# Fusing four transformer layers on one core: the second full attention's keys computed ahead of their stage and kept in DRAM

## The chip, the cores and the metric

The kernel runs on one core of a Trainium2 chip. The metric is device time in microseconds (us) of that core; the median of three runs stands below. The engines are TensorE (PE in the rows, its weight loads PEld), VectorE (DVE), ScalarE (ACT), GpSimd (POOL) and SyncE (SP), which only issues DMAs. ACTq and SPq are the DMA queues that ACT and SP issue to.

## The reference

Four layers follow each other over `x` of 8 rows (batch) x 128 tokens x 256 features, each an attention to a fixed context and a feed-forward block, with a residual sum and a layer norm ahead of both:

```python
x = x + _L0_xattn_ref(_layernorm(x), ctx_2048, ...)   # first cross attention, over 256 feature positions, 16 heads
x = x + _L0_ffn_ref(_layernorm(x), ...)               # first mixture of 8 experts, 2 chosen
x = x + _L1_xattn_ref(_layernorm(x), ctx_2048, ...)   # second cross attention
x = x + _L1_ffn_ref(_layernorm(x), ...)               # quantised feed-forward
x = x + _L2_xattn_ref(_layernorm(x), ctx_2048, ...)   # full attention, 16 heads of 128
x = x + _L2_ffn_ref(_layernorm(x), ...)               # low-rank mixture
x = x + _L3_xattn_ref(_layernorm(x), ctx_2048, ...)   # attention to memory
x = x + _L3_ffn_ref(_layernorm(x), ...)               # grouped attention, then the second mixture of experts

def _L2_xattn_ref(inputs_q, inputs_kv, Wq, Wk, Wv, Wo):
    q = (inputs_q @ Wq).reshape(b, sq, H, HD) * (1.0 / np.sqrt(HD))
    k = (inputs_kv @ Wk).reshape(b, skv, H, HD)
    v = (inputs_kv @ Wv).reshape(b, skv, H, HD)
    attn = jax.nn.softmax(jnp.einsum('bqhd,bkhd->bhqk', q, k), axis=-1)
    return jnp.einsum('bhqk,bkhd->bqhd', attn, v).reshape(b, sq, H * HD) @ Wo
```

The line that the change is about is `k = inputs_kv @ Wk`. Its `inputs_kv` is the context, an input of the whole program: these keys depend on nothing that is computed before them. They are 1024 tokens x 2048 columns in float32, 8.4 MB.

## The kernel before

Every engine has one program, written out by hand, that runs in order; engines meet at semaphores (`wait_ge`). PSUM is the tile `P` with eight banks of 512 words a lane. `big1`, `big2`, `big3` and `small` are areas of SBUF that each stage lays out anew; `X` holds the residual rows, `XN` the normalised ones, `XNT` and `CT` the transposed rows and the transposed context. The stages, in order of time:

- **First cross attention** (0 to 195 us). `s0_sp` loads and stacks, `s0_pe`, `s0_act`, `s0_dve` and `s0_pool` walk over `STEPS`. A step is one head `h` of 16 of one row `n` of 8. In each step PE writes `scores(n, h)` into bank 0 or 1 (L305), DVE takes their maximum (L480), and 24 steps later (`LEAD = H + 8`) PE computes the same product the other way round, `turned(m, g)` (L323), ACT takes its exponential (L556), and every fourth step PE weighs the values with it, `weigh` (L341), and once a row places the sums, `place` (L353). In the first 24 steps there are thus only `scores`, besides `project` (L286, L287) at h = 2 and `values` (L295) at h = 6. The queries and keys of a row go out to DRAM split in three bf16 parts (`split_out`, L256) and come back as stacks of lanes (`s0_stack`, L247 and L249, twelve DMAs a row); mask lanes follow (`s0_extra`, L234), and one row of ones goes through `SCR1` (L531, L534). The maxima go back to the stacks in `max_rows` (L516, DMAs that ACT issues).
- **Routing of the first mixture** (195 to 226 us). `s1_pe` turns the normalised rows and forms the gate logits (L148, L157), DVE chooses experts (L714 to L967), PE counts ranks (`ranks_pe`, L804 to L809), turns the shares (L827), forms the bias rows (L831) and the slots (`slots_pe`, L814). Then the gathers, `turn` (L848), and the experts' loop, `up` (L858) and `down` (L868), 23 blocks with 2 MB of weights each, to about 430 us.
- **Second cross attention and its feed-forward** (to about 541 us).
- **Full attention with the low-rank mixture and the attention to memory** (`s47_pe`, 541 to about 860 us). One step `m` of 32 is one group of four heads (`b, g = divmod(m, 4)`). In step m PE runs, in this order: `scores4(m + 1)` (L1807), `queries4(m + 2)` (L1782), `turn_probs4(m)` (L1815), `keys4(m + 2)` (L1789), a piece for a later layer's row (`second`, L1841 and L1865), `output4(m - 1)` (L1834), `values4(m + 1)` (L1798), another piece (`third`, L1884 and others), `weigh4(m)` (L1822). ACT copies queries and keys out of PSUM (`copy_qk4`, L2116 and L2117), takes exponentials (L2124) and copies the turned probabilities (L2132); DVE finds maxima, scales (L2310) and copies the values (L2295) and the weighed sums (L2315), and keeps the residual rows and layer norms (L126 to L134).
- **Grouped attention** (the same function's second loop, to about 1150 us), of the same shape with other pieces, and then the second mixture.

A float32 matrix product of the source shows as two MATMUL records. A **pair**, below, is the keys of one head (128 columns) for 512 tokens (four of the eight rows): two products, one for each half of the 256 features, into one bank. 16 heads and two groups of rows make 32 pairs.

## Time and profile before

| | us |
|---|---|
| median of 3 runs | 1279.91 (1278.62 to 1280.27) |
| span of the profiled execution | 1275.9 |
| PE busy | 1085.1 (85% of the span) |
| DVE busy | 704.5 (55%) |
| ACT busy | 503.4 (39%) |
| POOL busy | 319.7 (25%) |

The span is that of the one execution that was profiled, from its first to its last instruction. It is 4.0 us under the median, which is what lies around the span; differences worked out in the span are carried over to the median as they are. PE's busy time is a union of overlapping records, so a stretch in which PE is busy all the time may be read as one in which it is the bound. The granted TensorE clock is given as a share of full speed (1.0 is 2.4 GHz, 0.5 is 1.2 GHz).

### The profile page before, as it was taken

The page shows a single profiled execution, that of the slowest core. Times are in us where ns is not written, and L with a number is a line of the kernel's source. Part 1 is how long each engine was busy: PE and PEld are TensorE (multiplying, and loading weights), DVE is VectorE, ACT ScalarE, POOL GpSimd, SP SyncE. Part 2 cuts the span into 40 slices and gives each one's busy share as a digit, 9 for nine tenths or more (in the row PEclk, how much of TensorE's full clock was granted, in tenths as well). Part 3 has the DMA queues.
Part 4 walks back from the last instruction along what each step waited for, and adds up shares of the span by engine and source line. Part 5 has one row for each costly group of instructions (what it writes and reads, how often), then busy time and mean ns, then how long its engine had stood idle before and what let it go on. Part 6 is the DMA issues. An engine that isn't in the chain of part 4 may idle for free.

```text
span 1275.9 us, 20612 instructions
## 1 busy us (share of the span) xinstructions
PE 1085.1 (85%) x7154; PEld 830.8 (65%) x7170; DVE 704.5 (55%) x1700; ACT 503.4 (39%) x1785; POOL 319.7 (25%) x440
## 2 busy tenths in 40 slices
PE   1788886999996788799999999996788999984784
PEld 0355444899995566588888888884555666653463
DVE  5777756212223788854554455555656666665334
ACT  0165561233231466644333333342445555542121
POOL 5544211122322355510000000002222222210562
PEclk9699996899997799999999999998989999997797
DMA  6443207899882070000000000040000000000785
GB/s 185 133 129 110 84 32 237 301 327 334 315 322 79 10 256 1 2 28 20 1 1 1 1 1 1 34 133 1 1 1 9 5 6 5 5 4 24 238 250 177
DMA packets 59731, 121.31 MB, mean 95 GB/s; under 512 B 9049, under 2 KB 37481, under 8 KB 53713
## 3 DMA queue, kind: packets, MB, share of 16 engines
q1 hardware_dynamic: 52217, 106.62, 25.0%
q0 software_dynamic: 4416, 12.06, 2.8%
q10 hardware_dynamic: 2996, 1.32, 0.4%
q8 instruction: 58, 0.95, 0.3%
q14 instruction: 44, 0.36, 0.1%
HBM read 107.29 MB, written 12.49 MB: 94 GB/s over the span
## 4 chain that ended last, share of the span: by engine, by line
PE 60%; DVE 17%; issue 8%; ACT 7%; DMA 4%; POOL 2%; SPq 1%; another core or an unknown queue 1%; ACTq 0%; DVEq 0%; POOLq 0%
PE P L858 6%; PE P L868 6%; PE P L1789 4%; PE P L1782 4%; PE P L1834 4%; PE P L1798 4%; ACT big L2213 3%; DVE small L480 2%; PE P L1927 2%; PE P L1807 2%; PE P L1822 2%; PE P L1933 2%; PE P L1978 2%; ACT big L2181 2%; PE P L341 1%
## 5 line engine op out<-in xcount | busy, mean ns | idle before, releaser
L139 POOL TENSOR_TENSOR lrs<-lve,mhalf 128x1 f32<-128x1 f32 x64 | 36.6, 572 | 364.5 <-DVE lve L130 332.4
L480 DVE TENSOR_REDUCE small<-P 128x2 f32<-128x512 f32 x128 | 83.3, 681 | 38.9 <-PE P L305 38.2
L2124 ACT ACTIVATE big<-P,small 128x128 f32<-128x128 f32 x128 | 45.2, 366 | 145.0 <-DVE small L2304 145.0
L897 ACT ACTIVATE big<-P,big 128x128 f32<-128x128 f32 x184 | 52.5, 368 | 125.3 <-PE P L858 112.4
L556 ACT ACTIVATE big<-P 128x512 f32<-128x512 f32 x128 | 72.0, 598 | 58.6 <-PE P L323 53.6
L858 PE MATMUL P<-big 128*128 128x128 f32 x736 | 88.2, 279 | 0.1
L858 PEld LDWEIGHTS P<-big 128*128 128x128 f32 x736 | 86.1, 196 | 1.0 <-DMA big<-b_w 0.5
L868 PE MATMUL P<-big 128*128 128x256 f32 x368 | 83.1, 379 | 0.0
L305 PE MATMUL P<-big 90*128 90x256 bf16 x256 | 54.9, 303 | 32.9 <-DMA big<-scr_qk 17.5
L2295 DVE COPY big<-P 128x512 f32<-128x512 f32 x32 | 22.1, 692 | 107.2 <-PE P L1798 107.2
L999 DVE COPY big<-P 128x256 f32<-128x256 f32 x23 | 9.8, 425 | 125.3 <-PE P L868 125.3
L2443 DVE TENSOR_TENSOR big<-P,big 128x512 f32<-128x512 f32 x40 | 27.6, 690 | 87.3 <-ACT big L2181 87.2
L868 PEld LDWEIGHTS P<-big 128*128 128x128 f32 x368 | 68.2, 190 | 8.4
L1978 PE MATMUL P<-big 128*128 128x256 f32 x256 | 64.1, 396 | 0.4 <-DVE big L2498 0.4
L1782 PE MATMUL P<-XNT,big 128*128 128x128 f32 x512 | 62.6, 275 | 0.0
L1789 PE MATMUL P<-CT,big 128*128 128x128 f32 x512 | 62.4, 275 | 0.0
L1927 PE MATMUL P<-big,XNT 128*128 128x512 f32 x128 | 61.4, 603 | 1.2 <-DVE big L2445 1.2
L305 PEld LDWEIGHTS P<-big 90*128 90x128 bf16 x256 | 20.3, 103 | 62.7 <-DVE small L480 29.1
L1933 PEld LDWEIGHTS P<-idf,big 128*128 128x128 f32 x288 | 35.7, 147 | 39.0 <-issue 22.7
L1834 PE MATMUL P<-big 128*128 128x256 f32 x256 | 60.6, 380 | 0.0
L1798 PE MATMUL P<-big,CT 128*128 128x512 f32 x128 | 60.2, 592 | 0.0
L1782 PEld LDWEIGHTS P<-XNT,big 128*128 128x128 f32 x512 | 59.7, 192 | 0.2 <-issue 0.2
(388 smaller groups left out, 2584.2 us busy)
## 6 DMA issues: line engine op xcount, KB each, us to landing
big<-b_w SPq DMA_DIRECT2D x23, 1028.0 KB
big<-b_w SPq DMA_DIRECT2D x23, 1024.0 KB
big<-scr_qk SPq DMA_DIRECT2D x96, 96.0 KB
big<-i_wgu SPq DMA_DIRECT2D x23, 352.0 KB
big<-moe_y SPq DMA_DIRECT2D x16, 256.0 KB, 4.2
big<-i_wd SPq DMA_DIRECT2D x23, 176.0 KB
scr_qk<-big SPq DMA_DIRECT2D x8, 384.0 KB
moe_x<-XN SPq DMA_DIRECT2D x16, 128.0 KB
```

Source lines behind the costliest of these rows:

```text
L305: t = pe.matmul(P[:, h % 2, c * D:c * D + D], QS[n % 3][0:90, h, c * 128:c * 128 + 128], KS[n % 3][0:90, h, :], start=True, stop=True)
L480: dve.tensor_reduce(negM[:, h, :], P[:, h % 2, :].rearrange("p (c s) -> p c s", c=2), AX.X, ALU.max, negate=True).then_inc(a_max, 1)
L556: act.activation(ER[:, g % 8], P[:, second_bank(i), :].rearrange("p (c t) -> p c t", c=2), ACT.Exp).then_inc(a_e, 1)
L858: m = pe.matmul(P[:, 2 * (j % 2) + f // 4, f % 4 * 128:f % 4 * 128 + 128], w1x[j % 3][:, k * F0 + f * 128:k * F0 + f * 128 + 128], xgT[j % ...
L868: m = pe.matmul(P[:, 6 + j % 2, 0:D], hT[j % 2][:, f, :], w2x[j % 3][:, f, :], start=(f == 0), stop=(f == FC - 1))
L1782: pe.matmul(P[:, 0, j * T:j * T + T], e_wqk[:, g, 0, k, j * 128:j * 128 + 128], XNT[:, k, b * T:b * T + T], start=(k == 0), stop=(k == KD ...
L1789: t = pe.matmul(P[:, 1, j * T:j * T + T], e_wqk[:, g, 1, k, j * 128:j * 128 + 128], CT[:, k, b * T:b * T + T], start=(k == 0), stop=(k == ...
L1798: t = pe.matmul(P[:, 2, :], CT[:, k, b * T:b * T + T], e_wvs[:, g, k, :], start=(k == 0), stop=(k == KD - 1))
L1834: t = pe.matmul(P[:, 7, 0:D], e_o[:, j, :], e_wos[:, 4 * g + j, :], start=(g == 0 and j == 0), stop=(g == 3 and j == 3))
L1927: t = pe.matmul(P[:, 0, :], XNT[:, k, b * T:b * T + T], h_wqs[:, g, k, :], start=(k == 0), stop=(k == KD - 1))
L1933: t = pe.transpose(P[:, bank, j * T:j * T + T], src[:, j, :], idf[:, :])
L1978: t = pe.matmul(P[:, 7, 0:D], h_o[:, j, :], h_wos[:, 4 * g + j, :], start=(g == 0 and j == 0), stop=(g == 3 and j == 3))
```

## The change

The keys of the full attention are no longer computed in their stage (`keys4` and the second copy of `copy_qk4` are gone). They are computed in 32 pairs at the start of the program, copied from PSUM to one of four slots in `XNT` (`k_out`) by ACT (`key_take`), stored from there to a DRAM tensor `KEYS` by a DMA that ACT issues (`key_store`, 256 KB in pieces of 512 bytes), and read back by SP as one 1 MB tile a row (`key_row`) into two buffers. The pairs stand at four places of PE's program: 8 ahead of the first `scores`, 12 as halves in the first 24 steps, 6 as halves at h = 5 and h = 10 of the rows 2 to 7, 3 behind the gate logits and 3 ahead of the first `turn`. A pair waits for the copy of an earlier one out of its bank (`k_ev`), a copy for the store of four pairs before it (`k_st`). Some semaphores are used twice, under new names with an offset (`k_pe` is `e_y`, `k_ev` is `f_ex`), which is why the rows below show these names.

To make room, other work is moved. The transposed context is loaded at the start and not with the first mixture's constants. The loads of the later rows of `x`, of the context, of the mask and of `selm` move behind: half of `x` to ACT's queue, behind the first key store, and the rest to SP's, between the store of a row's parts and the wait for it (`s0_behind`), together with the mask lanes of rows 1 and 2, which ACT issued before. In the full attention the queries have two SBUF buffers in place of one for queries and one for keys; the output weights of the grouped attention are loaded last.

```diff
+        k_wts = big1[:, 12288:16384].rearrange("p (g k n) -> p g k n", g=4, k=KD)
+        k_out = [XNT[:, s // 2, 512 * (s % 2):512 * (s % 2) + 512] for s in range(4)]
+        KEYS = nc.dram_tensor("keys_t", (B, 128, 4, 4, T), F32, kind="Internal").ap()
+        KP, K0, K1, K2 = 32, 8, 20, 26
+        def key_place(p):
+            g, rest = divmod(p, 8)
+            return g, rest // 4, rest % 4
+        def key_bank(p):
+            return 2 + p % 2 if p < K1 else 5 if p < K2 else (2, 3, 0, 0, 7, 6)[p - K2]
+        def key_weights(eng, g):
+            eng.dma_start(k_wts[:, g], e_wk.rearrange("(k p) n -> p k n", p=128)[:, :, 512 * g:512 * g + 512]
+                          ).then_inc(k_w[g], 16)
+        def key_take(act, p):
+            act.wait_ge(k_pe, p + 1)
+            if p >= 4:
+                act.wait_ge(k_st[p % 4], 16 * (p // 4))
+            act.activation(k_out[p % 4], P[:, key_bank(p), :], ACT.Copy).then_inc(k_ev, 1)
+        def key_store(act, p):
+            g, r, j = key_place(p)
+            act.wait_ge(k_ev, p + 1)
+            act.dma_start(KEYS[4 * r:4 * r + 4, :, g, j].rearrange("b p t -> p b t"),
+                          k_out[p % 4].rearrange("p (b t) -> p b t", b=4)).then_inc(k_st[p % 4], 16)
+        def key_part(pe, p, lo, hi):
+            g, r, j = key_place(p)
+            if lo == 0:
+                if p % 8 == 0:
+                    pe.wait_ge(k_w[g], 32 if g == 0 else 16)
+                if p == 4:
+                    pe.wait_ge(k_ct, 16)
+                if K1 <= p < K2:
+                    pe.wait_ge(k_ev, p)
+                elif 2 <= p < K1:
+                    pe.wait_ge(k_ev, p - 1)
+                elif p == K2 + 3:
+                    pe.wait_ge(k_ev, p)
+            for k in range(KD):
+                t = pe.matmul(P[:, key_bank(p), lo:hi], k_wts[:, g, k, 128 * j:128 * j + 128],
+                              CT[:, k, 512 * r + lo:512 * r + hi], start=(k == 0), stop=(k == KD - 1))
+            if hi == 512:
+                t.then_inc(k_pe, 1)
+        def late_pair(n, h):
+            if 2 <= n < B and h in (5, 10):
+                return K1 + n - 2, h // 10
+            return None
...
+            sp.dma_start(X[:, 2:4, :], x_cbt[:, 2:4, :]).then_inc(ld_x, 16)
+            ctx_t = ctxT.rearrange("(k p) n -> p k n", p=128)
+            sp.dma_start(CT[:, :, 0:512], ctx_t[:, :, 0:512]).then_inc(k_w[0], 16)
+            key_weights(sp, 0)
+            sp.dma_start(CT[:, :, 512:NT], ctx_t[:, :, 512:NT]).then_inc(k_ct, 16)
...
+            if n == 1:
+                sp.dma_start(TMf[:, 2 * D:], rows(mask.rearrange("b d -> (b d)").rearrange("(a n) -> a n", a=1)[:, 2 * D:])
+                             ).then_inc(a_ldm, 16)
+                sp.wait_ge(a_exd, 32)
+            if n in (1, 2):
+                for half in range(2):
+                    s0_extra(sp, n, half)
+            if n == 1:
+                key_weights(sp, 2)
+            if n == 2:
+                sp.dma_start(CX[:, 4:8, :], ctx.rearrange("b c t -> c b t")[:, 4:8, :]).then_inc(ld_c2, 16)
+                sp.dma_start(selm, a_sel).then_inc(a_ldm, 16)
+                key_weights(sp, 3)
...
+            for p in range(K0):
+                key_part(pe, p, 0, 512)
...
+                if step < LEAD:
+                    key_part(pe, K0 + step // 2, D * (step % 2), D * (step % 2) + D)
+                if late_pair(n, h) is not None:
+                    p, u = late_pair(n, h)
+                    if n + 2 < B and h == 5:
+                        pe.wait_ge(a_qb, n + 3)
+                    key_part(pe, p, D * u, D * u + D)
...
+            key_take(act, 0)
+            key_store(act, 0)
+            act.dma_start(X[:, 4:8, :], x.rearrange("b c t -> c b t")[:, 4:8, :]).then_inc(ld_x2, 16)
+            key_take(act, 1)
+            key_store(act, 1)
+            key_weights(act, 1)
             act.wait_ge(a_exd, 32)
-            for n in range(3):
-                for half in range(2):
-                    s0_extra(act, n, half)
+            for p in range(2, K0):
+                if p in (2, 4):
+                    s0_extra(act, 0, p // 2 - 1)
+                key_take(act, p)
+                key_store(act, p)
...
+                if step < LEAD and step % 2:
+                    key_take(act, K0 + step // 2)
+                    key_store(act, K0 + step // 2)
+                if 2 <= n < B and h == 11:
+                    key_take(act, late_pair(n, 10)[0])
+                if 2 <= n < B and h == 13:
+                    key_store(act, late_pair(n, 10)[0])
...
+            rows_logits_pe(pe, 1, gw, (b_ld, 80), b_lt)
+            for p in range(K2, K2 + 3):
+                key_part(pe, p, 0, 512)
...
+            for p in range(K2 + 3, KP):
+                key_part(pe, p, 0, 512)
             pe.wait_ge(b_acc, 4)
             turn(0)
             turn(1)
+            pe.wait_ge(k_ev, KP)
             up(0)
...
+        def key_row(sp, b):
+            if b >= 2:
+                sp.wait_ge(e_s, 4 * (b - 2) + 4)
+            sp.dma_start(e_kr[b % 2], KEYS[b]).then_inc(k_rd[b % 2], 16)
         def s4_sp(sp):
             sp.wait_ge(xn_ready, 3 * B)
-            for w, src in enumerate((e_wq, e_wk)):
-                for g in range(4):
-                    sp.dma_start(e_wqk[:, g, w], src.rearrange("(k p) n -> p k n", p=128)[:, :, 512 * g:512 * g + 512]
-                                 ).then_inc(e_ld, 16)
+            for signal in k_st:
+                sp.wait_ge(signal, 16 * KP // 4)
+            wq4 = e_wq.rearrange("(k p) n -> p k n", p=128)
+            sp.dma_start(e_wqs[:, 0], wq4[:, :, 0:512]).then_inc(e_ld, 16)
+            key_row(sp, 0)
+            for g in range(1, 4):
+                sp.dma_start(e_wqs[:, g], wq4[:, :, 512 * g:512 * g + 512]).then_inc(e_ld, 16)
             for g in range(4):
                 sp.dma_start(e_wvs[:, g], e_wv.rearrange("(k p) n -> p k n", p=128)[:, :, 512 * g:512 * g + 512]
                              ).then_inc(e_ld, 16)
             sp.dma_start(e_wos, e_wo.rearrange("(h p) d -> p h d", p=128)).then_inc(e_ld, 16)
+            key_row(sp, 1)
...
-            def keys4(m):
-                b, g = divmod(m, 4)
-                for j in range(4):
-                    for k in range(KD):
-                        t = pe.matmul(P[:, 1, j * T:j * T + T], e_wqk[:, g, 1, k, j * 128:j * 128 + 128],
-                                      CT[:, k, b * T:b * T + T], start=(k == 0), stop=(k == KD - 1))
...
+                if g == 0:
+                    pe.wait_ge(k_rd[b % 2], KRD0 + 16 * (b // 2) + 16)
...
-                if m + 2 < NM:
-                    keys4(m + 2)
...
-                act.activation(e_q.rearrange("p j t -> p (j t)"), P[:, 0, :], ACT.Copy)
-                act.activation(e_k.rearrange("p j t -> p (j t)"), P[:, 1, :], ACT.Copy).then_inc(e_qkT, 1)
+                if m >= 2:
+                    act.wait_ge(e_s, m - 1)
+                act.activation(e_q[m % 2].rearrange("p j t -> p (j t)"), P[:, 0, :], ACT.Copy).then_inc(e_qkT, 1)
```

The opening, PE, from its first product on, before. L286 and L287 are `project`, L305 is `scores`:

```order
L286 MATMUL P<-XN,small 128x256 [waits a_ld,xn_ready]
L287 MATMUL P<-CX,small 128x256
L286 MATMUL P<-XN,small 128x256 [waits a_qb,xn_ready]
L287 MATMUL P<-CX,small 128x256
L305 MATMUL P<-big 128x256 [waits a_stk00]
L305 MATMUL P<-big 128x256 x3
L305 MATMUL P<-big 128x256 [waits a_max]
```

and with the change, where L368 and L369 are `project`, L387 is `scores` and L259 a key product:

```order
L368 MATMUL P<-XN,small 128x256 [waits a_ld,xn_ready]
L369 MATMUL P<-CX,small 128x256
L368 MATMUL P<-XN,small 128x256 [waits a_qb,xn_ready]
L369 MATMUL P<-CX,small 128x256
L259 MATMUL P<-CT,big 128x512 [waits c_ld]
L259 MATMUL P<-CT,big 128x512 x3
L259 MATMUL P<-CT,big 128x512 [waits f_ex]
L259 MATMUL P<-CT,big 128x512
L259 MATMUL P<-CT,big 128x512 [waits f_ex]
L259 MATMUL P<-CT,big 128x512
L259 MATMUL P<-CT,big 128x512 [waits f_ex,i_ld]
L259 MATMUL P<-CT,big 128x512
```

Between the second `project` and the first `scores` there are now the 16 products of eight pairs (the rows shown are the first four of them), and each pair from the third on waits for `f_ex`, the count of copies.

The opening, ACT, before (L504 and L505 copy the projections, L524 and L525 store the mask parts, L234 is `s0_extra`):

```order
L504 ACTIVATE big<-P,small 128x256 [waits a_qkf,a_qk]
L505 ACTIVATE big<-P,small 128x256
L524 DMA scr_e<-big 8x4608 [waits a_exs]
L525 DMA scr_e<-big 8x4608
L234 DMA big<-scr_e 18x8x256 [waits a_exd]
L234 DMA big<-scr_e 18x8x256 x11
L531 DMA scr<-big 3x4096 [waits a_one]
L534 DMA big<-scr 3x4096 [waits a_exd]
```

and with the change (L235 is `key_take`, L241 `key_store`, L311 `s0_extra`):

```order
L623 DMA scr_e<-big 8x4608
L235 ACTIVATE XNT<-P 128x512 [waits e_y]
L241 DMA keys_t<-XNT 128x4x128 [waits f_ex]
L626 DMA X<-x 128x4x256
L235 ACTIVATE XNT<-P 128x512 [waits e_y]
L241 DMA keys_t<-XNT 128x4x128 [waits f_ex]
L227 DMA big<-e_wk 128x2x512
L311 DMA big<-scr_e 18x8x256 [waits a_exd]
L311 DMA big<-scr_e 18x8x256
L235 ACTIVATE XNT<-P 128x512 [waits e_y]
L241 DMA keys_t<-XNT 128x4x128 [waits f_ex]
L235 ACTIVATE XNT<-P 128x512 [waits e_y]
```

ACT's copies of the third pair and of all later ones stand behind its wait for `a_exd` and behind the mask lanes; the last of the eight stores is directly ahead of the store of ones and its wait.

One step of the full attention, PE, before, from `scores4` to `weigh4` (names in the section above):

```order
L1807 MATMUL P<-big 128x128 x4
L1782 MATMUL P<-XNT,big 128x128 x8
L1815 MATMUL P<-idf,big 128x128 x4
L1789 MATMUL P<-CT,big 128x128 x8
L1865 MATMUL P<-idf,big 128x128
L1834 MATMUL P<-big 128x256 x4
L1798 MATMUL P<-big,CT 128x512 x2
L1890 MATMUL P<-big 128x256
L1822 MATMUL P<-big 128x128 x4
```

and with the change, the same step:

```order
L1953 MATMUL P<-big 128x128 x4
L1932 MATMUL P<-XNT,big 128x128 x8
L1962 MATMUL P<-idf,big 128x128 x4
L2012 MATMUL P<-idf,big 128x128
L1981 MATMUL P<-big 128x256 x4
L1941 MATMUL P<-big,CT 128x512 x2
L2037 MATMUL P<-big 128x256
L1969 MATMUL P<-big 128x128 x4
```

The eight products of `keys4` are gone from between `turn_probs4` and the piece behind it; the other work of the step is in the same order.

## Rows read from the trace of the kernel before

**Rows 1.** The page's head.

```profile
span 1275.9 us, 20612 instructions
```

**Rows 2.** Windows: length; busy us (x instructions) of each engine; granted clock; DMA share; GB/s.

```profile
8.00:14.00 6.00, 4.09 (x8) 2.35 (x8) 5.86 (x10) 1.59 (x5) 2.55 (x3) 1.00 1.00 294
14.00:30.00 16.00, 0.00 (x0) 0.00 (x0) 7.57 (x21) 0.29 (x1) 11.65 (x11) 1.00 0.54 165
...
95.50:113.70 18.20, 15.72 (x145) 9.67 (x145) 13.88 (x28) 10.19 (x21) 8.96 (x14) 1.00 0.35 106
625.00:850.00 225.00, 225.00 (x1546) 196.07 (x1545) 116.59 (x345) 79.91 (x303) 13.00 (x27) 1.00 0.05 15
905.00:1145.00 240.00, 215.56 (x992) 143.91 (x1004) 156.05 (x355) 127.40 (x592) 51.78 (x87) 0.99 0.01 4
```

**Rows 3.** Groups by line: shape, count; busy us, mean ns; idle before.

```profile
L1789 PE MATMUL P<-CT,big 128*128 128x128 f32 x512 | 62.4, 275 | 0.0
...
L1798 PE MATMUL P<-big,CT 128*128 128x512 f32 x128 | 60.2, 592 | 0.0
```

**Rows 4.** Timeline, full attention: start, length, engine, line [idle before it].

```profile
707.61 1.95 PE L1789 MATMUL P<-CT,big 128*128 128x128 f32 x16
...
709.13 0.61 ACT L2132 ACTIVATE big<-P 128x512 f32<-128x512 f32 x1
...
709.39 0.27 PE L1865 MATMUL P<-idf,big 128*128 128x128 f32 x1
...
713.38 1.05 PE L1822 MATMUL P<-big 128*128 128x128 f32 x8
...
716.74 0.41 DVE L134 TENSOR_SCALAR XN<-X,lmv,lrs 128x256 f32<-128x256 f32 x1
...
719.39 0.38 PE L1841 MATMUL P<-idf,XN 128*128 128x128 f32 x2
```

**Rows 5.** Timeline, the opening.

```profile
12.35 1.06 PE L287 MATMUL P<-CX,small 128*128 128x256 f32 x2
...
16.41 0.39 SPq L256 DMA_DIRECT2D scr_qk<-big  x1
...
21.25 0.81 SPq L247 DMA_DIRECT2D big<-scr_qk  x1
...
21.68 8.18 ACTq L234 DMA_DIRECT2D big<-scr_e  x12
...
30.89 1.03 PE L305 MATMUL P<-big 90*128 90x256 bf16 x4 [17.47 <-DMA big<-scr_qk]
...
37.87 0.47 ACT L504 ACTIVATE big<-P,small 128x256 f32<-128x256 f32 x1 [23.58 <-DMA big<-scr]
```

**Rows 6.** Timeline, PE: the first `turned`, and `scores` at either clock.

```profile
56.34 0.61 PE L323 MATMUL P<-big 93*128 93x256 bf16 x2 [0.53 <-DMA big<-small]
...
63.61 0.38 PE L305 MATMUL P<-big 90*128 90x256 bf16 x2
63.83 0.38 PE L323 MATMUL P<-big 93*128 93x256 bf16 x2
```

**Rows 7.** Windows, the stretch around them.

```profile
55.00:60.00 5.00, 4.23 (x19) 2.43 (x20) 4.73 (x8) 2.05 (x4) 4.71 (x6) 0.50 0.45 132
```

**Rows 8.** Timeline, PE: `place` in a row of the steady part.

```profile
77.52 1.99 PE L353 MATMUL P<-big,small 128*128 128x256 f32 x8 [0.73 <-ACT big L540]
```

**Rows 9.** Timeline, PE: the routing of the first mixture.

```profile
199.10 1.66 PE L148 MATMUL P<-small,XNT 128*128 128x8 f32 x8
...
205.69 0.23 PE L804 MATMUL P<-big,small 128*128 128x64 bf16 x1 [4.93 <-DVE big L728]
...
224.78 1.23 PE L848 MATMUL P<-idf,big 128*128 128x128 f32 x4 [5.26 <-DMA big<-moe_x,big]
...
226.05 5.84 PE L858 MATMUL P<-big 128*128 128x128 f32 x32
...
231.94 3.74 PE L858 MATMUL P<-big 128*128 128x128 f32 x32
```

More of the change, by code:

```diff
@@ L884, in s1_act @@
         def s1_act(act):
+            for i in range(4):
+                act.wait_ge(k_st[i], 16 * len(range(i, K2, 4)))
             transposes_act(act, 1)
             gates_act(act, 0)
+            for p in range(K2, K2 + 3):
+                key_take(act, p)
+                key_store(act, p)
             act.wait_ge(b_cT, 1)
@@ L890, in s1_act @@
             t.then_inc(b_cTs, 1)
+            for p in range(K2 + 3, KP):
+                key_take(act, p)
+                key_store(act, p)
             for j in range(NB):
@@ L976, in s1_dve @@
             shares_of(dve, 0, 0.0)
-            step, weights_of = route_dve(dve, b_pos, POS0, b_rank, RANK0, b_ld, 128)
+            step, weights_of = route_dve(dve, b_pos, POS0, b_rank, RANK0, b_ld, 112)
             weights_of()
@@ L1712, in build @@
         CLEAR = 6
+        ld_x2, FLD0 = f_ld, 16
+        ld_c2, MLD0 = m_ld, 16
+        a_ldm, HLT0 = h_lt, 32
+        k_w, CLD0, ELD0, HLD0, HLD20 = [c_ld, e_ld, h_ld, h_ld2], 32, 16, 16, 16
+        k_ct, ILD0 = i_ld, 16
+        k_pe, EY0 = e_y, KP
+        k_ev, FEX0 = f_ex, KP
+        k_rd, KRD0 = [ld_c, ld_id], 16
+        h_ld3, HLD30 = a_ldv, 48
         def again(eng, sems):
@@ L1990, in turn_fed @@
                     t.then_inc(tb_pe, 1)
-            pe.wait_ge(e_ld, 208)
+            pe.wait_ge(e_ld, ELD0 + 144)
             pe.wait_ge(tb_ev, TURNED[B - 1])
             queries4(0)
-            keys4(0)
             output2(B - 1)
@@ L2001, in s47_pe @@
             queries4(1)
-            keys4(1)
             for m in range(NM):
@@ L2658, in build @@
         i_w = [sem("i_w0"), sem("i_w1"), i_z] + b_w
-        IW0 = [0] * 3 + [32 * len(range(u, NB, 3)) for u in range(3)]
+        IW0 = [16 * KP // 4] * 3 + [32 * len(range(u, NB, 3)) for u in range(3)]
         i_xs = b_xg + [a_stk[2][0], a_stk[2][1], e_max, e_bias, e_rz, e_pn]
         NG = len(i_xg)
+        k_st, MY0 = i_w[:3] + [m_y], 16 * KP // 4
         IXS0 = [16 * len(range(u, NB, 4)) for u in range(4)] + [0] * 6
```

108 lines of the change are left out of this document (63 added, 45 removed).

## The prediction, made before the changed kernel was run

> **What bounds the kernel now.** I read the windows first, stage by stage, and for each asked whether PE is ever idle. In the full attention it is not: of the 225 us from 625 to 850 PE is busy for 225.00, at the full clock, with DVE at 116.59 and ACT at 79.91 [rows 2]. Whatever is taken from PE there comes off the end, until another engine's chain is late. The grouped attention, of the same shape, is the warning: PE is busy for 215.56 of 240 us [rows 2], so there such chains do show. In the first cross attention PE is busy for 15.72 us of a row of 18.20, DVE for 13.88 [rows 2]; no engine is the bound alone, and they hand the path to each other. Ahead of it PE does nothing from 14 to 30 us [rows 2] and waits 17.47 us for the first stacks [rows 5], and in the routing it waits 4.93 us for DVE and 5.26 us for the first gather [rows 9]. The change moves PE work from the stage without holes to the places with holes. The sum is what it takes off less what does not fit in the holes.
>
> **The full attention: keys4 gone.** Its groups of records show 62.4 us for 512 [rows 3], 1.95 us a step, but the last record's tail overlaps what follows. From start to start the keys take 709.39 - 707.61 = 1.78 us [rows 4], and 32 steps give 57.0 us. What could be late when they no longer lie between `turn_probs4` and the rest? I moved the later rows of the step forward by 1.78 and looked at who feeds them. `weigh4`, at 713.38, would start at 711.60; it needs ACT's copy L2132, done at 709.13 + 0.61 = 709.74, 1.9 us to spare [rows 4]. The piece at 719.39 would start at 717.61; its input is the layer norm's L134, done at 717.15, 0.46 us to spare [rows 4]. What stands ahead of `turn_probs4` keeps its distance from it. ACT loses a copy a step. The read of a key row (1 MB, 8 KB pieces) is released five steps ahead of its use, some 40 us; at the 294 GB/s that the full share of 8 to 14 us moves it takes 3.6 us, and DMA is at a share of 0.05 in this stage [rows 2]: nothing. I allow 2.5 us for pieces that come late now and for the first two steps, where `scores4(1)` stands right behind the queries that it needs. **Term: -54.5** (bounds -57, and -29 as worked out in the first rival).
>
> **What a pair costs.** Products of 512 columns take 60.2 us for 64 [rows 3], less a tail of 0.16 a pair as above: 1.72 us a pair. A half of 256 columns I take at half of it. All this holds at full clock, and twice as much at half.
>
> **The opening: 20 pairs.** The second `project` ends at about 13.2 us [rows 5], and the weights and the first half of the context (1.3 MB behind 0.9 MB, at 294 GB/s) are there by 12 or 13. Eight pairs take 13.8 us at full clock, and the hole up to 30.89 [rows 5] is 17.7. But ACT gates them: its third copy stands behind the wait for the mask parts (21.68 before [rows 5]) and two mask-lane DMAs of 0.68 each (8.18 for 12 [rows 5]), so the fifth pair starts at about 24.5 and the eighth ends at about 32. First `scores`: 1.3 us later than before. Then 24 steps of 0.22 us for `scores` (63.61 to 63.83 [rows 6]), twelve pairs and 2.6 us of `project` and `values` (six 256-column products' worth at 0.43): 28.5 us of PE work, which DVE's reductions do not limit. Into this falls one wait: the copy of the ninth pair stands behind the store of ones and its return. Before, that took from the end of the mask lanes at 29.86 to 37.87 [rows 5], 8.0 us; now it begins at about 33, so PE, which wants that bank at about 38, waits until about 42. The 24 steps end at 65 in place of 56.34 [rows 6]: +8.7. Against this, the clock. Before, the first `turned` takes 0.61 us for what takes 0.38 later, and the window around it is at a granted 0.50 [rows 6, 7]; with PE at work without a hole from 13 us on I expect full clock there, which gives back 2 us. DMA: the mask, `x` and context loads move, but some 8.4 MB (5.2 of stores, 2 of weights, 1 of context) are new ahead of 65 us, 28 us of all 16 engines at 294 GB/s; the stretch to 65 goes from about half busy (0.54 in 14 to 30 [rows 2]) to 0.9. I take 2 us for it. **Term: +9** (bounds +3, all the stalls hidden, to +20).
>
> The Trainium skill, DMA: Bandwidth & Descriptors, section "Issuing engines are not separate DMA queues", says that DMAs of ACT and SP run on the same 16 engines and interleave, so a second issuing engine saves issue time only. No row here shows two queues at a full share together; by it the stores slow the stacks of SP's queue (the second rival), and were the queues apart, the term would be +7.
>
> **Six late pairs.** 10.3 us of PE work in six rows. The half at h = 10 stands where `place` waits 0.73 us for ACT [rows 8] and costs 0.1 to 0.2; the half at h = 5 waits for ACT's `queries_keys`, and behind that ACT issues the three DMAs of `max_rows`, which PE has to wait out anyway. PE has 18.20 - 15.72 = 2.5 us a row idle [rows 2] for 1.72. ACT's copy and store issue (1.1 us) fall where DVE is late. Between nothing and 10.3 I take **+4**, nearer to nothing because of the idle time.
>
> **The routing.** Three pairs (5.2 us) start when the logits end, at 199.10 + 1.66 = 200.8, and ranks start at 205.69 [rows 9]: +0.3 to +1. Three more stand ahead of the first `turn`, where PE waits 5.26 us for the gather [rows 9], a hole for 5.2 us at full clock, 10.3 at half. But `up` took 5.84 us there [rows 9], at half clock at first, against 3.74 for the 32 records of the next block [rows 9]; warmed, it gives 2 us back. **Term: +1** (bounds -1, +6). Six stores (1.6 MB) beside the experts' weights: **+0.5** (0 to 3). ACT's waits for `k_st` at stage borders find the stores landed.
>
> **Sum.** -54.5 + 9 + 4 + 1 + 0.5 = -40. On the span: 1275.9 [rows 1] to about 1236; on the median, 4.0 us above it: **1240**. The terms' likely errors together are some 10 us: 1228 to 1252.
>
> **Rivals.**
> 1. *The full attention finds a new bound.* If DVE's or ACT's chain limits it as in the grouped attention, PE is busy for 0.898 of the time (215.56 / 240 [rows 2]). Of the 309 us from 541 to 850, 252 of work remain; at 0.898 that is 281, so 28 of 57 come off: 1240 + 26 = 1266. For it: 0.46 us to spare above, and DVE's share rises to 116.59 / (225 - 41) = 0.63 [rows 2]. Against: the waits of the grouped attention are at rows that its other chain of queries brings. Chance 0.09.
> 2. *DMA bounds the opening.* If stores in 512-byte pieces move at half the 294 GB/s, 5.2 MB take 35 us in place of 18, and with about 30 of before and 10 of loads the 65 us become 76: +11, 1251, with late pairs at full price up to 1258. For it: the window at 8 to 14 us is already at share 1.00 [rows 2]. Chance 0.14.
> 3. *The clock stays at half in the first 24 steps* as in the window at 0.50, though PE was busy 4.23 of 5 us there [rows 7]: 28.5 us become 57, less 4 of stall: +25, 1265. Against: PE's stream is now denser than there, with products of 512 columns. The Trainium skill, TensorE: Matmul & The Clock Gate, Part 1, says that the throttled state is the default and activity releases it; by it this rival does not happen, and the trace agrees as far as the clock rises once `turned` joins `scores` [rows 6]. Chance 0.03.
> 4. *Slower than before: the four store slots.* The copy of pair p waits for the store of pair p - 4. A store of 384 KB landed in 21.25 - 16.41 = 4.8 us [rows 5]; four pairs take 6.9 us, so it is hidden. Were a store to take 25 us, sixteen pairs in four rounds would take 100, and the 24 steps end at 117: +58 for the opening, 1290. It decides from about 23 us on. Chance 0.04.
>
> **How the numbers follow.** Forecast 0.70 (1228 to 1252), rivals 0.09, 0.14, 0.03, 0.04. Range: 1226 to 1260, with the second rival in and the first, third and fourth (0.16) out, and a little below. A measurement tells 0.2% (2.6 us) from no change. Faster by more: all but the fourth and some mishap beyond the rows, 0.93; within 0.02; slower 0.05.
>
> **What would show it.** A step of the full attention 8.0 us long (9.7 before, 309 us for 32), PE without idle time; if it is idle before `turn_probs4` or the normalised rows, the first rival. The first `turned` near 65 us, at full clock, with waits of PE for ACT's copies near 24 and 40 us. A row of the steady part 0.7 us longer. Ranks within 1 us behind DVE's choice. A time over 1260 means a chain in the full attention that I did not see; one under 1226 that the opening's waits were no waits at all.

## The result and the profile after

| | before | with the change |
|---|---|---|
| median, us | 1280.25 (1278.62 to 1281.8) | 1271.65 (1268.04 to 1274.83), 5 runs |
| ratio | 1 | 0.9922 (0.9897 to 0.9946) |
| span of the profiled execution, us | 1275.9 | 1270.8 |

The change makes the kernel 0.8% faster: 8.6 us on the median, 5.1 us between the two profiled spans. Forecast was 40, and 1271.65 lies outside the range. The starts of a few first instructions in the two traces show where the difference arises. The shift is how much later an instruction comes than before, and its growth is what the stretch that ends there costs.

| first instruction of | before | after | shift | growth | forecast |
|---|---|---|---|---|---|
| `scores` | 30.9 | 40.1 | +9.2 | | +1.3 |
| `turned` | 56.3 | 90.1 | +33.8 | +33.8 | +9 |
| the gate logits | 194.9 | 233.2 | +38.3 | +4.5 | +4 |
| `up` | 226.1 | 268.6 | +42.5 | +4.2 | +1 |
| `queries4` | 540.0 | 583.0 | +43.0 | +0.5 | +0.5 |
| the grouped attention's `turn` | 874.9 | 870.8 | -4.1 | -47.1 | -54.5 |
| end of the span | 1275.9 | 1270.8 | -5.1 | -1.0 | 0 |

Of the five terms of the sum two failed: the opening by 25 us, the full attention by 7. Late pairs and the stores beside the experts' weights came as forecast, the routing 3 us dearer, inside its bounds. The windows of after, with the columns of [rows 2] (length; busy of PE, PEld, DVE, ACT, POOL with counts; granted clock; DMA share; GB/s):

```profile
14.00:30.00 16.00, 11.85 (x24) 4.23 (x22) 7.51 (x21) 2.64 (x5) 11.62 (x11) 1.00 0.70 198
30.00:50.00 20.00, 12.42 (x38) 6.98 (x38) 3.46 (x5) 2.39 (x4) 0.00 (x0) 0.83 0.85 224
50.00:60.00 10.00, 1.12 (x3) 0.94 (x4) 0.00 (x0) 1.19 (x2) 0.00 (x0) 0.50 0.29 103
60.00:90.00 30.00, 25.12 (x132) 19.83 (x130) 19.86 (x41) 8.42 (x16) 14.81 (x20) 0.90 0.71 213
...
660.00:850.00 190.00, 181.83 (x1143) 150.69 (x1142) 112.66 (x336) 66.83 (x274) 12.45 (x26) 1.00 0.12 41
```

The 17.47 us hole ahead of the first stacks [rows 5] is filled, as meant: PE is busy for 11.85 us from 14 to 30, where it was at 0.00. But a new hole stands at 50 to 60 us, in which PE works for 1.12 us and its granted clock goes to 0.50. In the full attention PE, busy without a gap before [rows 2], is idle for 8.2 of 190 us. The waits of PE in these two stretches (line waited at, releaser: us in total, times, longest), first 14 to 95, then 660 to 850 us:

```profile
PE P L259 <- ACT XNT L235: 20.6, 5, 11.8
PE P L407 <- DMA big<-small: 5.0, 1, 5.0
```

```profile
PE P L1988 <- ACT XNT L2280: 7.6, 5, 1.5
```

L259 is the key product, L235 ACT's copy `key_take`, L407 `turned`, L1988 the transposes of a late piece. The longest wait and the first `turned`, where [rows 6] had a wait of 0.53:

```profile
58.88 2.08 PE L259 MATMUL P<-CT,big 128*128 128x256 f32 x4 [11.76 <-ACT XNT L235]
...
90.11 0.61 PE L407 MATMUL P<-big 93*128 93x256 bf16 x2 [4.98 <-DMA big<-small]
```

What kept ACT is in its own timeline. L241 is `key_store`, L311 the mask lanes, L637 and L640 the store of ones and the three reads of it; the second number of a DMA row is how long the issue held the engine:

```profile
25.47 1.15 ACTq L241 DMA_DIRECT2D keys_t<-XNT  x1
26.65 6.12 ACTq L311 DMA_DIRECT2D big<-scr_e  x2
...
35.03 3.00 ACTq L241 DMA_DIRECT2D keys_t<-XNT  x1
38.29 0.60 ACT L235 ACTIVATE XNT<-P 128x512 f32<-128x512 f32 x1 [3.29 <-DMA keys_t<-XNT]
...
43.17 0.60 ACT L235 ACTIVATE XNT<-P 128x512 f32<-128x512 f32 x1 [4.28 <-DMA keys_t<-XNT]
...
44.20 5.13 ACTq L637 DMA_DIRECT2D scr<-big  x1
57.21 0.91 ACTq L640 DMA_DIRECT2D big<-scr  x3
58.23 0.60 ACT L235 ACTIVATE XNT<-P 128x512 f32<-128x512 f32 x1 [14.46 <-DMA big<-scr]
```

Three different things hold ACT here. First, the issuing itself: two mask-lane DMAs take 6.12 us (12 of them took 8.18 before [rows 5]), one key store 3.00, the store of ones 5.13. Second, copies wait for slots, 3.29 and 4.28 us. Third, from the issue of the ones' store to its return 13.0 us pass (44.20 to 57.21), where I had counted 8. All of them stand behind key stores. A store has 512 pieces of 512 bytes and lands late, as the page and the account of its line show (min/median/max over all 32):

```profile
q10 hardware_dynamic: 19468, 10.17, 2.9%
...
keys_t<-XNT ACTq DMA_DIRECT2D x32, 256.0 KB, 10.2
```

```profile
DMA to landing us min/median/max: 2.3/10.2/17.6
```

q10 is ACT's queue: 19468 packets and 10.17 MB (before: 2996 and 1.32). Whether it is the pieces, the bytes, the slots or the ones' trip, the trace doesn't say, since each holds ACT in turn.

### The profile page after: what moved, and what is told of

It is laid out like the page before. It is cut to its first block, busy times and chain, and to the rows that moved or that the text cites. A ratio compares the mean times of both kernels' runs of the same rounds, so it can differ in the third digit from the quotient of the medians.

```text
span 1270.8 us, 20090 instructions
## 1 busy us (share of the span) xinstructions
PE 1086.5 (85%) x6858; PEld 811.3 (64%) x6858; DVE 705.5 (56%) x1700; ACT 505.7 (40%) x1785; POOL 320.0 (25%) x440
## 3 DMA queue, kind: packets, MB, share of 16 engines
q10 hardware_dynamic: 19468, 10.17, 2.9%
## 4 chain that ended last, share of the span: by engine, by line
PE 57%; DVE 19%; issue 8%; ACT 7%; DMA 6%; POOL 1%; ACTq 1%; another core or an unknown queue 0%; SPq 0%; DVEq 0%; POOLq 0%
PE P L974 6%; PE P L984 6%; PE P L1981 4%; PE P L1941 4%; PE P L259 3%; PE P L1932 3%; ACT big L2357 3%; PE P L2074 2%; PE P L2882 2%; DVE small L576 2%; PE P L426 2%; PE P L2080 2%; PE P L387 2%; DVE big L2589 1%; PE P L2127 1%
## 5 line engine op out<-in xcount | busy, mean ns | idle before, releaser
L662 ACT ACTIVATE big<-P 128x512 f32<-128x512 f32 x128 | 72.7, 599 | 58.8 <-PE P L407 52.3
L259 PE MATMUL P<-CT,big 128*128 128x256 f32 (+1 forms) x200 | 74.9, 508 | 21.6 <-ACT XNT L235 20.6
L259 PEld LDWEIGHTS P<-CT,big 128*128 128x128 f32 x200 | 39.3, 215 | 46.2 <-ACT XNT L235 22.6
L2080 PE MATMUL P<-idf,big 128*128 128x128 f32 x288 | 46.2, 286 | 15.6 <-DVE big L2642 9.3
L2366 ACT ACTIVATE big<-P 128x512 f32<-128x512 f32 x32 | 19.1, 598 | 100.4 <-PE P L2080 100.1
## 6 DMA issues: line engine op xcount, KB each, us to landing
keys_t<-XNT ACTq DMA_DIRECT2D x32, 256.0 KB, 10.2
```

The source lines that it names most:

```text
L259: t = pe.matmul(P[:, key_bank(p), lo:hi], k_wts[:, g, k, 128 * j:128 * j + 128], CT[:, k, 512 * r + lo:512 * r + hi], start=(k == 0), stop ...
L662: act.activation(ER[:, g % 8], P[:, second_bank(i), :].rearrange("p (c t) -> p c t", c=2), ACT.Exp).then_inc(a_e, 1)
L2080: t = pe.transpose(P[:, bank, j * T:j * T + T], src[:, j, :], idf[:, :])
```

## The experiments

The chips differ by 0.7% in the time of the kernel before (1272.07, 1271.18 and 1280.42 us in the three jobs), so the ratios are compared and not the times. "First `turned`" and other starts are of the profiled executions.

**No pairs at all.** All `key_part`, `key_take` and `key_store` calls and their waits are left out; the moved loads, those of the keys' weights (2 MB) and the read of 1 MB a row stay. The keys are left out: what is read in their place is a weight tensor.

```diff
-        KP, K0, K1, K2 = 32, 8, 20, 26
+        KP, K0, K1, K2 = 0, 0, 0, 0
-            sp.dma_start(e_kr[b % 2], KEYS[b]).then_inc(k_rd[b % 2], 16)
+            sp.dma_start(e_kr[b % 2], e_wk[0:128, :].rearrange("p (g j t) -> p g j t", g=4, j=4)
+                         ).then_inc(k_rd[b % 2], 16)
```

> The change without any early key work: no pairs on TensorE, no copies on ScalarE, no stores; the moved loads, the mask lanes on SyncE's queue and the whole of the full attention stay as changed, and the key rows are read (same bytes, same pieces) from a weight tensor. It leaves the keys out, so the time is that of the rest. In the two traces the full attention became 47 us shorter and everything ahead of it 43 us longer. If the 43 us are all key work, this kernel takes 1271.7 - 43 = 1229 us, and the moved loads cost nothing. The rival, that the moved loads (mask, context, half of x behind other transfers) cost a part of it, gives 1235 or more.

Measured: 0.9653 (0.9627 to 0.9679), first `turned` at 64.2: the rival of the expectation. All the key work together thus takes back 2.7% of the 3.5% that the rest of the change brings, and the new and moved loads alone cost 7.9 us of the opening (64.2 - 56.3) without a single pair. The 3.5% is not a ceiling: the waits in the full attention are still in this kernel (262.7 us from the first `queries4` to the last, as in the changed one).

**Pairs and copies, but no stores** (`key_store` only waits for its copy, and the waits for a slot are gone with the stores; the same reads as above).

```diff
             act.wait_ge(k_ev, p + 1)
-            act.dma_start(KEYS[4 * r:4 * r + 4, :, g, j].rearrange("b p t -> p b t"),
-                          k_out[p % 4].rearrange("p (b t) -> p b t", b=4)).then_inc(k_st[p % 4], 16)
```

> The change with all 32 pairs and all copies, but without the 32 stores and without the waits for them; the key rows are read from a weight tensor. It leaves out the storing of the keys. Theory A (the stores hold up ScalarE's queue and the slots, and what is issued behind them): the wait of 11.8 us for the ones, the 5.3 us ahead of the eighth pair and most of the 5.0 us for the maxima go, 1245 to 1250 us. Theory B (the pairs and copies themselves do not fit into the holes): 1266 us or more.

Measured: 0.9748 (0.973 to 0.9767), first `turned` at 67.1: theory A. All of PE's and ACT's work on 20 pairs costs 2.9 us in the opening (67.1 - 64.2). The stores, with the waits for their slots, cost 1.7% of the time, 22 us, and 23.0 us of the first `turned` (90.1 - 67.1).

**Stores in pieces of 2048 bytes.** The same bytes, slots and order; the four rows of a store lie side by side in DRAM, which makes 128 pieces of it in place of 512. They are read back in pieces of 512 bytes.

```diff
-        KEYS = nc.dram_tensor("keys_t", (B, 128, 4, 4, T), F32, kind="Internal").ap()
+        KEYS = nc.dram_tensor("keys_t", (2, 128, 4, 4, 4, T), F32, kind="Internal").ap()
-            act.dma_start(KEYS[4 * r:4 * r + 4, :, g, j].rearrange("b p t -> p b t"),
+            act.dma_start(KEYS[r, :, g, j],
-            sp.dma_start(e_kr[b % 2], KEYS[b]).then_inc(k_rd[b % 2], 16)
+            sp.dma_start(e_kr[b % 2], KEYS[b // 4, :, :, :, b % 4]).then_inc(k_rd[b % 2], 16)
```

> The change with the DRAM tensor of the keys laid out so that a lane's 2 KB of a store are one piece instead of four of 512 bytes; the read back has the small pieces instead. Same bytes, same count of DMAs. Theory A1 (the count of pieces is what fills ScalarE's queue): stores land in about 5 us instead of 10, the opening loses 15 to 20 us, 1252 to 1257 us. Theory A2 (bytes fill the 16 DMA engines): no difference beyond 3 us, 1269 to 1273.

Measured: 0.9759 (0.9742 to 0.9775), first `turned` at 73.0: theory A1, and a little better. The same rows of ACT as above, and between them its wait for a slot:

```profile
25.66 1.54 ACTq L311 DMA_DIRECT2D big<-scr_e  x2
...
35.32 0.60 ACT L235 ACTIVATE XNT<-P 128x512 f32<-128x512 f32 x1 [6.34 <-DMA keys_t<-XNT]
...
37.37 0.35 ACTq L637 DMA_DIRECT2D scr<-big  x1
43.08 1.16 ACTq L640 DMA_DIRECT2D big<-scr  x3
```

The mask lanes issue in 1.54 us for 6.12, the ones in 0.35 for 5.13, and the ones' trip is 5.7 us for 13.0. It still has every byte and every wait of the changed kernel; the wait for a slot, 6.34 us, is even longer than the two of 3.29 and 4.28. Yet 17.1 of the 23.0 us in the opening are gone and about 21 of the 22 us in all. So it is the cut into many small pieces that costs them, and the bytes, the slots and the order together at most the 5.9 us that are left of the opening. With the same bytes, more pieces and smaller pieces are one thing. The layouts also differ in where the pieces lie (the lanes of a store are 8 KB apart in DRAM in the changed kernel, 32 KB here); no run separates that from the number.

**Only the ones' trip taken out**: its store moved ahead of the pairs' stores, its memset ahead of POOL's split.

```diff
-            split(0)
             pool.memset(onerow, 1.0).then_inc(a_one, 1)
+            split(0)
...
             act.dma_start(SCRE[:, 1], exk).then_inc(a_exd, 16)
+            act.wait_ge(a_one, 3)
+            act.dma_start(SCR1, onerow).then_inc(a_exd, 16)
             key_take(act, 0)
...
-            act.wait_ge(a_one, 3)
-            act.dma_start(SCR1, onerow).then_inc(a_exd, 16)
```

> The change with one thing moved: the store of ones is issued directly behind the mask parts (its memset on GpSimd ahead of the first split), its return is waited for together with theirs and loaded ahead of the third copy, so nothing waits for it behind eight key stores. If the 11.8 us wait in the first 24 steps is only a matter of where the ones stand in ScalarE's program: 1260 us. If the slots and the queue simply hold the next pairs as long (the stores as the bound of the opening): 1268 or more.

Measured: 0.9924 (0.9907 to 0.994), no gain over the changed kernel (0.9922 and, below, 0.9933); first `turned` at 87.7. The wait of 11.76 us is gone, but PE now waits 4.44, 1.51, 6.47 and 5.33 us for copies, 17.7 us in all for 20.6, the last of them for a copy that stands behind a slot and a key store of 5.18 us. The edit is not a clean one: with the memset ahead of the split, the mask parts are stored at 20.89 in place of 16.65, and the first `scores` comes at 45.6 in place of 40.1. So it shows only that this way of taking out the trip brings nothing; another one follows at the end.

**The changed kernel again**, on the chip of the next three:

> The changed kernel as it is, for a comparison on this chip with the others. Expected 0.992 of the kernel before, first `turned` near 90 us.

Measured: 0.9933 (0.9915 to 0.9952), first `turned` at 94.1. A start in the opening can thus differ by 4 us between profiles of the same kernel on two chips.

**The late piece of the memory's rows moved** behind `output4`, to test the full attention alone:

```diff
-                second(m)
+                if row_at(m, 8) is None:
+                    second(m)
...
                     output4(m - 1)
+                if row_at(m, 8) is not None:
+                    second(m)
```

> The changed kernel with one call moved: in the full attention `second(m)` of a step that carries a piece of the memory's rows stands behind `output4(m - 1)`, no longer right behind the step's first late piece. Theory A: the 7.6 us that PE waits for ACT's copy in 660 to 850 us come from two late pieces that use the same bank and between which `keys4` used to lie; with 0.8 us of other work between them the waits go and the time falls by 6 to 9 us (ratio to the kernel before 0.985 to 0.988 where the changed kernel stands at 0.992). Theory B: with `keys4` gone another chain (DVE's) bounds these steps; the wait then shows up under another line and the time stays within 2 us.

Measured: 0.9872 (0.9853 to 0.9891), 1254.73 us beside 1262.91 of the changed kernel on the same chip, 8.2 less: theory A. The window of 660 to 850 us:

```profile
660.00:850.00 190.00, 189.25 (x1174) 155.24 (x1173) 117.64 (x353) 70.55 (x297) 14.38 (x30) 1.00 0.15 51
```

PE is busy for 189.25 us in place of 181.83, and the wait for ACT's copy of the late piece is gone. From the first `queries4` to the last there are now 254.1 us (before 308.3, changed 262.7): -54.2, and -55.7 up to `turn`. Between this profile and that of the changed kernel on the same chip 8.5 us go in the full attention and 2.8 ahead of it, where nothing was edited, and 3.5 come back in the grouped attention, on which more below.

**Both edits together**, 2048-byte pieces and the moved piece:

> Both edits: the keys laid out in DRAM so that a store has 2048-byte pieces, and the moved `second(m)`. If the two costs are apart (opening, full attention), the gains add: 0.9759 less 0.006, so about 0.970 of the kernel before. If the time were held elsewhere, no better than 0.976.

Measured: 0.9744 (0.9725 to 0.9764), 1238.86 us beside 1271.18. This beats both the kernel before and the changed one. The gains don't add (0.970 was expected): the interval overlaps that of the 2048-byte pieces alone (0.9742 to 0.9775), so the time of the whole kernel doesn't show that the moved piece brings anything on top; its stage does. Between the profiles of this version and the one with 2048-byte pieces alone, 8.5 us go in the full attention (287.8 to 279.3 from `queries4` to `turn`), but 2.8 come back behind it and 1.4 ahead. In the grouped attention the waits are the same in the changed kernel and in the one with the moved piece; what differs is the granted clock, 0.98 where the profile takes 281 us (from the first record of its `turn` to the last) and 0.97 where it takes 285. All four profiles with the moved piece take 285; of the eight other profiles with the change in them seven take 281, and one, the first of the changed kernel, takes 285 without the edit. So the moved piece may itself cost about 3.5 us there. Why the clock is lower there, no run shows.

**And the weights 2 and 3 loaded behind the stacks**:

```diff
-            if n == 1:
-                key_weights(sp, 2)
...
-                key_weights(sp, 3)
...
                     s0_stack(sp, n, half)
+                if n > 0:
+                    key_weights(sp, n + 1)
```

> As the one with both edits, and the keys' weights 2 and 3 are loaded behind the stacks of their row in place of ahead of them. Theory A: what delays the first `turned` even without any pair (64.2 us against 56.3) is these loads: SP needs 4.8 us to issue one, which holds the second row's stacks, and the maxima's transfer takes 9.3 us in place of 4.6 beside the other. Then the first `turned` comes 3 to 6 us earlier than with both edits alone, and the time falls by as much. Theory B: the same bytes disturb the stacks wherever they stand, or pair 16 now waits for its weights: within 2 us of it, or slower.

Measured: 0.9754 (0.9734 to 0.9775), first `turned` at 72.7 beside 72.9: theory B, the place of these two loads doesn't matter here.

**Pieces of 1024 bytes**, the test of a price for each piece:

```diff
-        KEYS = nc.dram_tensor("keys_t", (B, 128, 4, 4, T), F32, kind="Internal").ap()
+        KEYS = nc.dram_tensor("keys_t", (2, 2, 128, 4, 4, 2 * T), F32, kind="Internal").ap()
...
-            act.dma_start(KEYS[4 * r:4 * r + 4, :, g, j].rearrange("b p t -> p b t"),
-                          k_out[p % 4].rearrange("p (b t) -> p b t", b=4)).then_inc(k_st[p % 4], 16)
+            act.dma_start(KEYS[r, :, :, g, j].rearrange("b p t -> p b t"),
+                          k_out[p % 4].rearrange("p (b t) -> p b t", b=2)).then_inc(k_st[p % 4], 16)
```

> The changed kernel with the keys laid out so that a store has 1024-byte pieces (256 of them) in place of 512-byte ones (512 of them); read back in 512-byte pieces, as in the run with 2048-byte pieces (128 of them). Theory A: the cost of the stores goes with the number of pieces that ACT's queue has to take. Without stores the ratio is 0.975, with 512-byte pieces 0.993: half the pieces would then give half of it, 0.983 to 0.985. Theory B: it is a fixed trouble below some size of piece, 2048 being enough and 1024 enough or not: 0.976 or 0.993.

Measured: 0.9846 (0.9825 to 0.9867), first `turned` at 82.3. Theory A; a threshold between 1024 and 512 or between 2048 and 1024 bytes (theory B) would have given 0.976 or 0.993. Side by side, with the starts of all profiles that have the same opening:

| stores | pieces of the 20 stores | ratio | first `turned` | waits of PE for L235, to 100 us |
|---|---|---|---|---|
| none | 0 | 0.9748 | 67.1 | 3.1 |
| 2048 bytes | 2560 | 0.9759 | 73.0, 72.9 | 5.0, 3.5 |
| 1024 bytes | 5120 | 0.9846 | 82.3 | 9.2 |
| 512 bytes | 10240 | 0.9922, 0.9933 | 90.1, 94.1, 90.6 | 20.6, 23.5, 21.0 |

All of the stores' cost divided by their pieces is 2.3 ns a piece (5.9 us / 2560), 3.0 (15.2 / 5120) and 2.2 to 2.6 (23.0 and 27.0 / 10240). That is an average over the opening and not a price of the single piece: from 2560 to 5120 pieces a further one costs 3.6 ns (9.3 us), from 5120 to 10240 1.5 to 2.3 (7.8 to 11.8 us). The bytes are the same in the last three lines. ACT's queue of the 1024-byte version in its page:

```profile
q10 hardware_dynamic: 11276, 10.17, 2.5%
...
keys_t<-XNT ACTq DMA_DIRECT2D x32, 256.0 KB, 8.2
```

**No pairs, and the keys' weights not loaded either** (four loads of 512 KB; no keys are read here either):

```diff
-            key_weights(sp, 0)
...
-                key_weights(sp, 2)
...
-                key_weights(sp, 3)
...
-            key_weights(act, 1)
```

> As the run without pairs, copies and stores, and without the four loads of the keys' weights too (2 MB); the moved loads of the mask, of `x` and of the context stay. No key is computed, so the full attention works on wrong keys. Theory A: the weights' loads, one of which keeps SP for 4.8 us, delay the first `turned` from 56.3 to 64.2 us even without a pair; then it comes back to 57 to 59 and the ratio falls from 0.965 to about 0.960. Theory B: it is the moved loads (the mask's row for POOL, the late context): still 63 to 65.

Measured: 0.9638 (0.9612 to 0.9665) beside 0.9653, whose intervals overlap; first `turned` at 60.0. Between the theories, and on another chip than the run beside it: of the 7.9 us that the loads cost, 4.2 are the weights' and 3.7 those of the moved loads. Part of the latter is POOL's wait for the mask's row, which was loaded at the start before (start, length, engine, line, [idle]):

```profile
39.93 1.45 POOL L665 TENSOR_TENSOR big<-big 128x512 f32<-128x512 f32 x1 [0.88 <-DMA big<-mask]
...
59.98 0.61 PE L399 MATMUL P<-big 93*128 93x256 bf16 x2 [4.03 <-DMA big<-small]
```

and PE's wait of 4.03 us ahead of the first `turned` is for the maxima's transfer; it was 0.53 before [rows 6].

**The ones' trip taken out** of the version with 2048-byte pieces, the moved piece and the moved weights: the store of ones behind the weights 1 on ACT's queue, with a signal of its own, its reads ahead of the sixth copy.

```diff
             key_weights(act, 1)
+            act.wait_ge(a_one, 3)
+            act.dma_start(SCR1, onerow).then_inc(a_one, 16)
...
+                if p == 5:
+                    act.wait_ge(a_one, 19)
+                    for i in range(3):
+                        act.dma_start(KS[i][90:93, :, :].rearrange("p h t -> p (h t)"), SCR1).then_inc(a_exd, 16)
```

> The version with 2048-byte pieces, the moved `second(m)` and the weights 2 and 3 behind the stacks, and on top of it the store of ones right behind the weights 1 on ACT's queue, its three reads ahead of the sixth pair's copy. Theory A: the reads' wait no longer holds a copy, which takes PE's 4.8 us of waits for ACT's copies to about 3 and the first `turned` from 72.7 to about 71; ratio 0.973. Theory B: the maxima's path (DVE, POOL, the transfer) sets the first `turned`, and nothing changes: 0.974 to 0.976.

Measured: 0.9749 (0.9728 to 0.977), first `turned` at 72.3: nothing comes off, as theory B says. But this edit is not clean either. The first `scores` comes at 35.8 in place of 33.2, since copies wait behind the reads (PE waits 5.8 us in all for copies, 4.8 without the edit), and later PE waits for the weights 2, which it did not before:

```profile
58.40 1.13 PE L259 MATMUL P<-CT,big 128*128 128x256 f32 x4 [2.26 <-DMA big<-e_wk]
...
72.34 0.61 PE L406 MATMUL P<-big 93*128 93x256 bf16 x2 [3.63 <-DMA big<-small]
```

In both edits another wait took the place of the one that was taken out. What the ones' trip would cost alone stays open.

## Why the prediction was wrong, point by point

**The opening is the step that failed**: "I take 2 us for it", for some 8.4 MB of new transfers. I had divided bytes by the 294 GB/s of one window of large loads. The runs give 30.9 us in its place: 7.9 for the new and moved loads and 23.0 for the stores. The stores are 10240 pieces of 512 bytes, and that they are cut so small is 17.1 of the 23.0. The other 7 us of the term, PE's own work and its wait, measured 2.9. Together that is 33.8 for 9. The number of pieces was there to be worked out: the diff has `T` floats, 512 bytes, as the contiguous run.

**The second rival** (stores in 512-byte pieces at half rate) named the pieces, with a chance of 0.14 against 0.70 for a forecast that left them out, and was sized as time of all 16 engines: +11. Half rate is not what the pages show. The packets of ACT's queue take 2.9% of the span of 16 engines, 2.4% in the version with 2048-byte pieces and 0.5% without stores; so all 32 stores take 30.7 us of 16 engines' time in 512-byte pieces and 23.6 in pieces of 2048, 1.3 times and not twice as much. The 20 stores of the opening have about 4 of these 7 us, where the opening lost 17.1. What the rival missed is that the stores stand on the queue of an engine that has other work. ACT is held while it issues (6.12, 3.00 and 5.13 us), so the copies, PE's banks and the mask lanes all wait for it. DMA is at shares of 0.70 and 0.85 from 14 to 50 us but at 0.29 from 50 to 60, in the worst hole: the engines as a whole were not full there.

**The fourth rival's step**, "a store lands in 4.8 us, so it is hidden" by four slots, took its duration from a store alone on its queue [rows 5]. Key stores land in 10.2 us in the median and 17.6 at most, and copies do wait for them, 3.29 and 4.28 us. It did not reach the 23 us from which I had it decide.

**The pairs' own work** was rightly placed but for the wrong reason. I forecast the first `turned` near 65 from PE's sum; without stores it comes at 67.1. That closeness is luck: it comes at 64.2 without a pair, so the sum of PE's work is not what makes it 65. Loads cost 7.9 us, for which I had at most the 2 us of DMA, and the pairs 2.9, since PE had more idle time than I gave it credit for (without pairs it is busy for 18.81 of the 32.2 us from the first `scores` to the first `turned`).

**The clock.** Forecast was full clock in the first 24 steps. The window of 50 to 60 us is at 0.50, with PE at work for 1.12 us of it, and the first `turned` takes 0.61 us as before. In the version with both edits PE is busy for 10.00 of 10 us from 50 to 60, and at 1.00, so the expectation holds for that stretch. Even there the maxima's wait (4.60 us ahead of the first `turned`) is followed by the lower level:

```profile
50.00:60.00 10.00, 10.00 (x56) 7.88 (x55) 7.91 (x16) 2.77 (x5) 5.86 (x9) 1.00 0.85 255
...
72.00:74.00 2.00, 1.09 (x6) 0.78 (x7) 0.02 (x1) 0.45 (x1) 1.90 (x4) 0.59 0.64 232
74.00:76.00 2.00, 2.00 (x11) 1.44 (x10) 1.68 (x3) 1.35 (x3) 0.97 (x3) 0.50 0.79 231
```

**Two queues at once.** The prediction cited the Trainium skill, DMA: Bandwidth & Descriptors, section "Issuing engines are not separate DMA queues", by which DMAs of ACT and of SP share the 16 engines and interleave. The version with 2048-byte pieces agrees with it: SP issues its first stack at 21.16 us there and at 20.92 without stores, yet PE waits for a stack, which it doesn't without stores (first row with 2048-byte pieces, second without stores):

```profile
34.65 0.39 PE L387 MATMUL P<-big 90*128 90x256 bf16 x2 [2.99 <-DMA big<-scr_qk]
```

```profile
30.11 0.39 PE L382 MATMUL P<-big 90*128 90x256 bf16 x2
```

In the changed kernel itself the first `scores`, at 40.1, follows the eighth pair without a wait and tells nothing of the stacks. The first stacks count together with mask lanes that ACT issues, so these runs don't separate the shared engines from the blocked issuer.

**Full attention: -47.1 for -54.5.** The products taken out are worth what I counted: with the late piece moved it is -55.7 up to `turn`, where -54.5 was forecast. What failed is "what could be late": I went along one step and asked who feeds each piece. In every fourth step from the thirteenth on (five of 32) two late pieces go through bank 6 of PSUM: a transpose whose result ACT copies out, then the transposes of L1988 into the same bank. `keys4` lay between them and covered ACT's copy; now PE waits up to 1.5 us for it, 7.6 us in five waits. It is a wait for a bank and not for data, in steps that I had not read. The first rival (a new bound, -28) did not come: without that wait PE is busy for 189.25 of 190 us.

**Late pairs: +4.5 for +4**, and the wait at `place` [rows 8] went, as said. **Routing: +4.2 for +1.** The first three pairs and the ranks cost 2.9 (the ranks' shift is 41.2), the second three 1.3 more. Both take longer than the 5.2 us of full clock (the granted clock of 260 to 267 us is 0.65), so the gather's hole of 5.26 [rows 9] does not hold the second three:

```profile
238.95 8.12 PE L259 MATMUL P<-CT,big 128*128 128x512 f32 x12
...
259.81 7.94 PE L259 MATMUL P<-CT,big 128*128 128x512 f32 x12
```

That case was inside the term's bounds ("10.3 at half"). **Experts' weights beside the stores: +0.5 for +0.5.**

## What to carry to other kernels

When a change adds DMAs, count their contiguous pieces before their bytes, and look which engine issues them and what stands behind them on it: here stores of 10240 pieces cost 23 us, the same bytes in four times fewer pieces 6. When work is taken out from between two steps, ask not only who feeds what follows, but which buffers or banks its duration gave time to be emptied, in each kind of iteration. And the longest wait in a trace is not yet a cost: two edits took the ones' trip out, other waits took its place, and nothing was gained.

## What the runs showed of the hardware

I had not expected an issuing engine to be held for so long: 5.13 us by the store of ones and 3.00 by the sixth key store, which take 0.35 and 0.38 us in the version with 2048-byte pieces, and 6.12 by two mask-lane DMAs, which take 1.54 there. It happened behind four to eight stores of 512 pieces. SP was held as well, at one load of weights behind mask lanes and stacks, for 4.8 us without any pair or store, for 1.65 with the pairs but no stores, for 4.15 in the changed kernel and for 4.37 in the version with 2048-byte pieces:

```profile
33.75 4.37 SPq L227 DMA_DIRECT2D big<-e_wk  x1
```

So it is not a matter of ACT alone, nor of key stores alone. What in the queue is full then, these runs don't tell, nor how much of the price of a piece is the hold of the issuer and how much the transfer itself.
